# A new order of all four engines' operations in a batch attention

## The chip, the cores and the metric

The kernel runs on one core of a Trainium2 chip. The metric is the time of one execution on the device in microseconds; the lower the better. A core has four compute engines with instruction queues of their own: TensorE (PE for its matmuls, PEld for its weight loads), VectorE (DVE), ScalarE (ACT) and GpSimd (POOL); SyncE (SP) issues most of the DMAs. An engine runs its own list strictly in the order in which the program issued it, and lists meet only at semaphores: `wait_ge(sem, n)` holds an engine until the semaphore has reached n.

## What is computed

Two layers over 32 sequences of 256 tokens with 128 features, each block followed by a layer norm of the sum:

```python
x = _layernorm(x + _L0_attn_ref(x, ...))   # causal attention with relative positions, 16 heads
x = _layernorm(x + _L0_ffn_ref(x, ...))    # 14 routed experts, top 2, and 2 shared
x = _layernorm(x + _L1_attn_ref(x, ...))   # recurrence and feed-forward
x = _layernorm(x + _L1_ffn_ref(x, ...))    # attention over the batch, then 8 experts
```

Only the attention inside the last block matters here. It reads the 32 sequences as the sequence axis: at each of the 256 positions the 32 batch entries attend to one another, causally, with 16 heads of size 8.

```python
s, b, h = x.shape                    # 32, 256, 128
hn = layernorm(x, ln1_w, ln1_b)
q, k, v = jnp.split(hn @ in_proj_w.T + in_proj_b, 3, axis=-1)      # 16 heads of 8
scores = jnp.einsum('sbnd,tbnd->bnst', q, k) / np.sqrt(HEAD_DIM)   # 32 x 32, causal
probs = jax.nn.softmax(scores, axis=-1)
attn = jnp.einsum('bnst,tbnd->sbnd', probs, v).reshape(s, b, h)
x1 = x + attn @ out_proj_w.T + out_proj_b
hn2 = layernorm(x1, ln2_w, ln2_b)    # then router and experts
```

## The kernel before

The program is a row of stages with a barrier of all engines between them. The stage that is changed is `attend_batches` (lines 2623 to 3145). It starts near 1500 us of the span and ends near 1838.

**Groups and steps.** The work is cut into NT = 64 groups `g` of 128 rows (4 positions times 32 batch entries; NPG = 4). Four groups (SLOTS = 4) are a step `f`; there are STEPS = 16 steps, and `g = 4f + s`.

**What a step does once.** `prepare(f)` (ScalarE, line 2957) scales four groups of rows, `turn(f)` (TensorE, 2849) transposes them, `affine(f)` (ScalarE, 2962) makes `hn`. From `hn` come `value` (TensorE, 2871), queries (2855) and keys (2857), which are `project` before. `values_out` (ScalarE, 2993) copies the values, and SyncE's `spread_values` writes them to DRAM and reads them back in another layout; `place_values` (POOL, 2763) makes block-diagonal values of them in two halves. `place_queries` (ScalarE, 2968, four instructions) and `place_keys` (VectorE, 3055, four instructions) do the same for queries and keys.

**What each group does.** `scores` (TensorE: mask 2861, four products 2864) fills the one bank `s_bank`; `soften` (VectorE) takes the maxima (3068) and subtracts them (3070); `exponents` (ScalarE, 2980); `sums` (VectorE, 3061 and the reciprocal 3063); `normalise_probs` (POOL, 2752); `turn_probs` (TensorE, 2879) into the one bank `p_bank`; `probs_out` (ScalarE, 2976) into the one tile `prob_t`; `mix` (TensorE, 2888) into the one bank `o_bank`; `outputs_out` (ScalarE, 2987, four instructions); `output` (TensorE, 2901) into `x_bank`; `add` (VectorE, 3093), `spread` (3098) and `aggregate` (3102) for the moments.

**What follows a step.** POOL's `root` (2728, 2730), `normalise_rows` (2740) and `add_rows` (2734); TensorE's `turn_rows` (2821), ScalarE's `move_rows` (2998), TensorE's router `score` (2828, eight matmuls of eight columns, issued ahead of the output of a step's first group) and VectorE's `keep_logits` (3074). Once, at group 25, `bias_of_experts` runs 32 matmuls of one column (2842). In steps 8 to 15 POOL also scales one expert's weights (`scale_expert`, 2748). `centred`, `e_x`, `prob` and `recip` are double buffers by `g % 2`; `total` and `peak` are single.

**The order** is written out by hand, one `step` function for each engine. Before the change every engine does, for each of the four `s`, a fixed list: TensorE `turn_probs(g-2)`, `scores(g)`, something that the step needs once, `mix(g-2)`, `output(g-3)`. So the scores are two groups ahead of the mix. VectorE does `sums(g-1)` and then `soften(g)`. After the stage come `choose_pairs` and `route_pairs`, which run the experts.

## Time and profile before

| | us |
|---|---|
| median of 3 runs | 2099.05 (2094.2 to 2105.48) |
| the profiled execution | 2104.3 |
| its span, first to last instruction | 2102.6 |
| TensorE busy | 1784.8 (85%) |
| VectorE busy | 1420.5 (68%) |
| ScalarE busy | 1361.6 (65%) |
| GpSimd busy | 1058.8 (50%) |
| mean granted TensorE clock | 0.928 |

The span is some 1.7 us shorter than the time of the same execution. The shares are averages over stages with different limits, so what is said of the changed stage has to be read inside 1500 to 1838 us. Busy time is the time in which at least one instruction of the engine ran. In the timeline each line is a start, a length, the engine and line, and a count of instructions that were merged (`x8`); in square brackets stands the idle time of the engine just before and what ended it. TensorE's instructions overlap, so the distance from start to start, and not the length, says what one costs in a dense row. A float32 matmul stands as two instructions.

### The profile page before, as it was taken

The numbers are of one execution on the slowest core, as the hardware profiler recorded it, in microseconds if no ns is written. First come the engines' busy times: TensorE is split into PE (matmuls) and PEld (weight loads), VectorE is DVE, ScalarE is ACT, GpSimd is POOL, SyncE is SP. The second block draws the span as 40 slices with busy tenths as digits, with TensorE's granted clock in tenths as the row PEclk, the third lists the DMA queues.
The fourth block names the chain that finished last, engine by engine and source line by source line (L and its number), as shares of the span: only waits on it lengthen the run. The fifth ranks groups of instructions, "written<-read, shape, count | busy, mean of one in ns | idle before, by whom it ended". The sixth has DMA issues, their size and how long they took to land. (4 is left out here: it accounts for less than half of the span.)

```text
span 2102.6 us, 52029 instructions
## 1 busy us (share of the span) xinstructions
PE 1784.8 (85%) x15928; PEld 1447.8 (69%) x15928; DVE 1420.5 (68%) x5901; ACT 1361.6 (65%) x3347; POOL 1058.8 (50%) x1384
## 2 busy tenths in 40 slices
PE   7799999999999989889998488888589898748895
PEld 6555555555555558779998377777478888628884
DVE  1377888788787874764422589998377666586775
ACT  3478888888888853324454378887477666416774
POOL 2123333333333323236675788885467777717574
PEclk9799999999999999999999699999799888858998
DMA  7889999999999944025666112221311221258552
GB/s 219 273 275 314 315 307 315 309 314 315 312 312 311 314 149 161 1 64 174 180 198 168 48 45 61 60 60 42 86 35 25 48 46 26 50 83 228 163 183 72
DMA packets 222092, 350.11 MB, mean 167 GB/s; under 512 B 56928, under 2 KB 169568, under 8 KB 221312
## 3 DMA queue, kind: packets, MB, share of 16 engines
q1 hardware_dynamic: 187024, 305.34, 46.1%
q0 software_dynamic: 14144, 31.16, 6.1%
q10 hardware_dynamic: 20656, 10.29, 1.7%
q8 instruction: 137, 2.24, 0.5%
q14 instruction: 131, 1.07, 0.2%
HBM read 160.82 MB, written 144.67 MB: 145 GB/s over the span
## 5 line engine op out<-in xcount | busy, mean ns | idle before, releaser
L183 POOL TENSOR_SCALAR_AFFINE_SELECT heads_raw_relative<-heads_raw_relative 128x508 f32<-128x508 f32 x256 | 167.1, 677 | 502.5 <-ACT heads_raw_relative L568 461.9
L568 ACT COPY heads_raw_relative<-heads_rel_bank 128x768 f32<-128x768 f32 x247 | 198.9, 805 | 124.8 <-PE heads_rel_bank L463 124.6
L492 PE MATMUL attend_turn_bank<-ident,attend_score 128*128 128x128 f32 x1536 | 233.2, 288 | 20.6 <-ACT attend_prob_t L574 20.2
L492 PEld LDWEIGHTS attend_turn_bank<-ident,attend_score 128*128 128x128 f32 x1536 | 164.6, 142 | 118.0 <-ACT attend_prob_t L574 67.9
L574 ACT ACTIVATE attend_prob_t<-attend_turn_bank 128x384 f32<-128x384 f32 x512 | 225.2, 501 | 7.6 <-PE attend_turn_bank L492 7.6
L578 ACT ACTIVATE attend_score<-attend_score,attend_extreme 128x128 f32<-128x128 f32 x512 | 215.6, 421 | 9.0 <-DVE attend_extreme L625 8.7
L625 DVE CUSTOM_DVE_ANT_0 attend_score<-attend_score_bank,heads_relative 128x256 f32<-128x256 f32 x512 | 214.7, 419 | 0.0
L622 DVE CUSTOM_DVE_ANT_0 attend_score<-attend_score_bank,heads_relative 128x128 f32<-128x128 f32 x512 | 146.3, 286 | 77.9 <-PE attend_score_bank L463 51.0
L631 DVE TENSOR_SCALAR attend_score<-attend_score,attend_extreme 128x256 f32<-128x256 f32 x512 | 195.8, 382 | 0.0
L1422 POOL DMA_INDIRECT moe_route_rows_sb<-tokens,moe_taken x154 | 145.9, 948 | 70.1 <-PE moe_route_bank L1444 40.5
L463 PE MATMUL attend_score_bank<-heads_qk 32*128 32x256 f32 x1024 | 156.1, 381 | 0.0
L2583 POOL DMA_INDIRECT recur_got<-expert_out,moe_slots x128 | 137.0, 1070 | 32.1 <-issue 32.1
L463 PE MATMUL heads_rel_bank<-heads_e,heads_qk 32*128 32x256 f32 x988 | 150.8, 382 | 0.0
L460 PE MATMUL heads_rel_bank<-heads_e,heads_qk 32*128 32x128 f32 x988 | 122.9, 325 | 19.4 <-PEq L59 1.5
L1543 DVE COPY moe_route_y<-moe_route_bank 128x128 f32<-128x128 f32 x154 | 44.6, 291 | 130.1 <-PE moe_route_bank L1462 119.8
L460 PE MATMUL attend_score_bank<-heads_qk 32*128 32x128 f32 x1024 | 127.3, 325 | 0.0
L1963 ACT ACTIVATE duo_hid<-duo_hid_bank,duo_w_now 128x128 f32<-128x128 f32 x316 | 98.0, 366 | 40.6 <-PE duo_hid_bank L1924 35.5
L460 PEld LDWEIGHTS heads_rel_bank<-heads_e,heads_qk 32*128 32x128 f32 x988 | 75.2, 186 | 69.6 <-ACT heads_raw_relative L568 47.0
L1933 PE MATMUL duo_y_bank<-moe_w,duo_hid 128*128 x632 | 101.6, 285 | 16.3 <-ACT duo_hid L1963 16.0
L2752 POOL TENSOR_TENSOR batch_prob<-batch_e_x,batch_recip 128x512 f32<-128x512 f32 x64 | 67.1, 1049 | 77.8 <-DVE batch_recip L3063 77.5
L1924 PE MATMUL duo_hid_bank<-moe_z,duo_w_now 128*128 x632 | 103.6, 289 | 2.0 <-ACT moe_z L1956 0.7
L2888 PE MATMUL batch_o_bank<-batch_prob_t,batch_v_blocks 128*128 128x128 f32 x512 | 75.8, 294 | 29.6 <-ACT batch_prob_t L2976 29.6
(434 smaller groups left out, 5327.9 us busy)
## 6 DMA issues: line engine op xcount, KB each, us to landing
shear<-heads_raw_relative SPq DMA_DIRECT2D x128, 768.0 KB, 5.2
heads_relative<-shear SPq DMA_DIRECT2D x128, 768.0 KB, 5.6
duo_w_now<-moe_w SPq DMA_DIRECT2D x158, 129.0 KB
moe_route_w_now<-moe_w SPq DMA_DIRECT2D x154, 129.0 KB
expert_out<-moe_route_y ACTq DMA_DIRECT2D x38, 256.0 KB, 3.4
qk_heads<-heads_qk_out SPq DMA_DIRECT2D x32, 256.0 KB, 4.4
heads_qk<-qk_heads SPq DMA_DIRECT2D x128, 64.0 KB
pair_rows<-groups SPq DMA_DIRECT2D x16, 260.0 KB, 8.0
```

Of the source, the lines that this page charges most:

```text
L183: m = nc.gpsimd.affine_select(out=future, in_=future, compare_op=ALU.is_ge, fill=-BIG, base=1 - P, pattern=[[0, QUAD], [1, P - 1]], channe ...
L460: nc.tensor.matmul(bank[:, 0:P], q[:, 0:P], m[:, 0:P], start=True, stop=True)
L463: mm = nc.tensor.matmul(bank[:, P:W], q[:, P:T], m[:, P:W] if of_rel else m[:, 0:T], start=True, stop=True)
L492: mm = nc.tensor.transpose(bank[:, j * P:(j + 1) * P], score[:, (h - LAG) % RING, j * P:(j + 1) * P], c.ident[:, :])
L568: nc.scalar.copy(raw[:, ring, 2 * half:2 * half + 2, :], r_bank[:, :, 0:W]).then_inc(rel_moved, 1)
L574: nc.scalar.activation(prob_t[:, (h - LAG) % RING, :], bank_of(h)[:, 0:W], ACT.Exp).then_inc(exped, 1)
L578: nc.scalar.activation(score[:, h % RING, 0:P], score[:, h % RING, 0:P], ACT.Identity, bias=extreme[:, h % RING, 0:1], scale=-1.0).then_in ...
L622: nc.vector.tensor_tensor_reduce(score[:, row, 0:P], bank[:, 0:P], rel[:, quad, h % QUAD, 0:P], -SM_SCALE, 3.0e38, ALU.add, ALU.min, extre ...
L625: nc.vector.tensor_tensor_reduce(score[:, row, P:W], bank[:, P:W], rel[:, quad, h % QUAD, P:W], SM_SCALE, -3.0e38, ALU.add, ALU.max, extre ...
L631: nc.vector.tensor_scalar(score[:, h % RING, P:W], score[:, h % RING, P:W], extreme[:, h % RING, 1:2], None, ALU.subtract).then_inc(centre ...
L1422: nc.gpsimd.indirect_dma_start(rows_sb[:, s % TAKEN, :], None, c.tokens, bass.IndirectOffsetOnAxis(ex.taken[:, s // S, s % S:s % S + 1], 0 ...
L2583: nc.gpsimd.indirect_dma_start(got[t % GOT][:, m, :], None, c.expert_out[0:choice.slot_rows, :], bass.IndirectOffsetOnAxis(choice.slots[:, ...
```

## The change

Each engine's `step` gets a new list; no operation is added or left out.

- TensorE: `project` is split into `project_queries` and `project_keys`. In step f it issues the scores of 4f to 4f+3, the turns of probabilities of 4f-4 to 4f-1, and the mixes of 4f-5 to 4f-2, so that scores are up to four groups ahead of the mix. `turn` runs two steps ahead instead of one.
- ScalarE: `outputs_out` and `probs_out` of the last groups stand at the end of the step, around the last `exponents`; `affine` runs two steps ahead.
- VectorE: `soften` of one or two groups stands ahead of `sums`; both halves of `place_keys` stand together between `soften(g+2)` and `soften(g+3)`.
- POOL: `place_values` of a step is done in that step in one piece; `normalise_rows` runs in two pieces that lie a step apart; `add_rows` is moved behind a normalisation.
- New waits say what the old order had implied (`affine` on the last readers of `hn`, `exponents` on `normed`, `soften` on `exped`, `add_rows` on `rooted`), and `total` becomes two buffers.
- The steps run to STEPS + 2, so the work that lags behind is drained by the same lists with conditions.

The diff, cut to its core (the removed lists stand in the listing above):

```diff
-        peak, total = sb("peak", [P, NPG * HB]), sb("total", [P, NPG * HB])
+        peak, total = sb("peak", [P, NPG * HB]), [sb(f"total{u}", [P, NPG * HB]) for u in range(2)]
...
             def add_rows(q):
                 cols = slice(SLOTS * q, SLOTS * (q + 1))
+                pool.wait_ge(rooted, q + 1)
...
+            def normalise_probs(g):
+                u = g % 2
                 pool.wait_ge(recip_done, g + 1)
+                wait_past(pool, p_turned, g - 1)
...
+            def step(f):                                   # POOL
+                g, live = SLOTS * f, f < STEPS
+                if 3 <= f:
+                    normalise_rows(f - 3, 1)
+                if live:
+                    normalise_probs(g)
+                if 2 <= f:
+                    root(f - 2)
+                if live:
+                    place_values(f, 0)
+                    place_values(f, 1)
+                if 2 <= f < STEPS + 1:
+                    normalise_rows(f - 2, 0)
+                if live:
+                    normalise_probs(g + 1)
+                    add_bias(f)
+                    normalise_probs(g + 2)
+                if 2 <= f:
+                    add_rows(f - 2)
+                if 8 <= f < 8 + n:
+                    scale_expert(f - 8)
+                if live:
+                    normalise_probs(g + 3)
...
             def turn(f):
                 pe.wait_ge(z_ready, f + 1)
+                wait_past(pe, hn_ready, f)
...
+            def step(f):                                   # TensorE
+                g, live, more, back, late = SLOTS * f, f < STEPS, f + 1 < STEPS, 1 <= f <= STEPS, 2 <= f
+                if late:
+                    mix(g - 5)
+                if back:
+                    turn_probs(g - 4)
+                if late:
+                    output(g - 6)
+                if live:
+                    scores(g)
+                if more:
+                    project_queries(f + 1)
+                if back:
+                    mix(g - 4)
+                if late:
+                    output(g - 5)
+                if back:
+                    turn_probs(g - 3)
+                if live:
+                    scores(g + 1)
+                if back:
+                    output(g - 4)
+                    turn_probs(g - 2)
+                    mix(g - 3)
+                if live:
+                    scores(g + 2)
+                if more:
+                    project_keys(f + 1)
+                if back:
+                    output(g - 3)
+                if 3 <= f <= STEPS:
+                    turn_rows(f - 3)
+                if back:
+                    mix(g - 2)
+                    turn_probs(g - 1)
+                if live:
+                    scores(g + 3)
+                if f + 2 < STEPS:
+                    turn(f + 2)
+                if more:
+                    value(f + 1)
...
+            def affine(f):
                 act.wait_ge(turned, f + 1)
+                wait_past(act, q_made, f - 1)
+                wait_past(act, k_made, f - 1)
+                wait_past(act, v_made, f - 1)
...
+            def exponents(g):
+                u = g % 2
                 act.wait_ge(softened, soft(g, "centred"))
+                wait_past(act, normed, g - 1)
...
+            def step(f):                                   # ScalarE
+                g, live, more, back = SLOTS * f, f < STEPS, f + 1 < STEPS, 1 <= f
+                if back:
+                    probs_out(g - 3)
+                if live:
+                    exponents(g)
+                if more:
+                    place_queries(f + 1, 0)
+                    place_queries(f + 1, 1)
+                if f + 2 < STEPS:
+                    prepare(f + 2)
+                if back:
+                    outputs_out(g - 3)
+                    probs_out(g - 2)
+                if more:
+                    place_queries(f + 1, 2)
+                if live:
+                    exponents(g + 1)
+                if 3 <= f:
+                    move_rows(f - 3)
+                if live:
+                    exponents(g + 2)
+                if back:
+                    probs_out(g - 1)
+                    outputs_out(g - 2)
+                if more:
+                    place_queries(f + 1, 3)
+                if f + 2 < STEPS:
+                    affine(f + 2)
+                if more:
+                    values_out(f + 1)
+                if back:
+                    outputs_out(g - 1)
+                if live:
+                    probs_out(g)
+                    exponents(g + 3)
+                    outputs_out(g)
...
+            def soften(g):
+                u = g % 2
                 dve.wait_ge(s_made, g + 1)
+                wait_past(dve, exped, g - 1)
...
+            def step(f):                                   # VectorE
+                g, live, more, back, late = SLOTS * f, f < STEPS, f + 1 < STEPS, 1 <= f <= STEPS, 2 <= f
+                if late:
+                    add(g - 6)
+                if live:
+                    soften(g)
+                if late:
+                    add(g - 5)
+                    spread(g - 6)
+                if back:
+                    sums(g - 1)
+                if late:
+                    spread(g - 5)
+                    aggregate(g - 6)
+                if live:
+                    soften(g + 1)
+                if back:
+                    add(g - 4)
+                if live:
+                    sums(g)
+                if back:
+                    spread(g - 4)
+                if late:
+                    aggregate(g - 5)
+                if live:
+                    soften(g + 2)
+                if more:
+                    place_keys(f + 1, 0)
+                    place_keys(f + 1, 1)
+                if back:
+                    add(g - 3)
+                if live:
+                    soften(g + 3)
+                    sums(g + 1)
+                if back:
+                    aggregate(g - 4)
+                if live:
+                    sums(g + 2)
+                if back:
+                    spread(g - 3)
+                    aggregate(g - 3)
```

(The names of the engines behind `def step(f):` are put there for the reader.)

## Rows read from the trace of the kernel before

**Rows 1.** Busy time by stretch: length, then each engine busy, clock, DMA share, GB/s.

```profile
1623.73:1641.17 17.44, 15.72 (x124) 13.91 (x122) 13.41 (x32) 13.87 (x36) 14.52 (x15) 1.00 0.46 90
1686.90:1707.25 20.35, 18.50 (x122) 17.09 (x121) 13.65 (x34) 13.87 (x36) 15.46 (x16) 0.83 0.12 27
...
1516.12:1788.66 272.54, 244.09 (x1660) 221.63 (x1660) 190.16 (x452) 191.21 (x480) 198.06 (x188) 0.89 0.18 40
1828.30:1837.53 9.23, 5.54 (x32) 4.77 (x32) 2.84 (x13) 1.17 (x2) 4.28 (x5) 0.72 0.27 59
```

**Rows 2.** Timeline (start, length, engine, line): the one-column matmuls of group 25.

```profile
1640.35 3.63 PE L2842 MATMUL batch_x_bank<-batch_shift,moe_w 128*128 128x1 f32 x32
```

**Rows 3.** Timeline of TensorE's matmuls, in a stretch of clock 1.00.

```profile
1708.57 1.06 PE L2871 MATMUL batch_v_bank<-fixed_w_in,batch_hn 128*128 128x128 f32 x8
...
1711.18 1.05 PE L2888 MATMUL batch_o_bank<-batch_prob_t,batch_v_blocks 128*128 128x128 f32 x8
...
1712.08 0.39 PE L2901 MATMUL batch_x_bank<-fixed_w_out,batch_out_t 128*128 128x128 f32 x2
...
1712.30 0.60 PE L2879 MATMUL batch_p_bank<-ident,batch_prob 128*128 128x128 f32 x4
...
1712.73 0.38 PE L2861 MATMUL batch_s_bank<-batch_causal,batch_ident_bf 128*128 128x512 bf16 x1
...
1713.84 0.60 PE L2821 MATMUL batch_turn_bank<-ident,moe_z 128*128 128x128 f32 x4
```

**Rows 4.** Waits from 1540 to 1820 us: waiter, releaser, total, times, longest.

```profile
PE batch_o_bank L2888 <- ACT batch_prob_t L2976: 25.9, 17, 1.9
```

**Rows 5.** Timeline: router matmuls of one step, and mix and router of another.

```profile
1636.14 0.96 PE L2828 MATMUL batch_x_bank<-batch_router_now,batch_zt 128*128 128x8 f32 x8
...
1718.95 1.46 PE L2888 MATMUL batch_o_bank<-batch_prob_t,batch_v_blocks 128*128 128x128 f32 x8 [1.85 <-ACT batch_prob_t L2976]
...
1720.20 1.71 PE L2828 MATMUL batch_x_bank<-batch_router_now,batch_zt 128*128 128x8 f32 x8
```

**Rows 6.** Timeline at the stage's end: probability copy, mix, output copy.

```profile
1821.90 0.59 ACT L2976 COPY batch_prob_t<-batch_p_bank 128x512 f32<-128x512 f32 x1
...
1822.54 0.97 PEld L2888 LDWEIGHTS batch_o_bank<-batch_prob_t,batch_v_blocks 128*128 128x128 f32 x8 [0.96 <-ACT batch_prob_t L2976]
...
1823.74 1.06 ACT L2987 COPY batch_out_t<-batch_o_bank 32x128 f32<-32x128 f32 x4 [1.25 <-PE batch_o_bank L2888]
```

**Rows 7.** Timeline of ScalarE, without idle time between.

```profile
1707.92 1.26 ACT L2957 ACTIVATE batch_z<-groups 128x128 f32<-128x128 f32 x4
...
1709.09 1.05 ACT L2987 COPY batch_out_t<-batch_o_bank 32x128 f32<-32x128 f32 x4
...
1710.16 0.59 ACT L2976 COPY batch_prob_t<-batch_p_bank 128x512 f32<-128x512 f32 x1
...
1710.64 0.63 ACT L2980 ACTIVATE batch_e_x<-batch_centred 128x512 f32<-128x512 f32 x1
...
1711.17 0.58 ACT L2993 COPY batch_v_rows<-batch_v_bank 128x512 f32<-128x512 f32 x1
...
1711.63 0.79 ACT L2968 ACTIVATE batch_q_blocks<-batch_q_bank,batch_q_shift,batch_of_b 128x512 f32<-128x512 f32 x1
...
1712.31 1.05 ACT L2987 COPY batch_out_t<-batch_o_bank 32x128 f32<-32x128 f32 x4
```

**Rows 8.** Timeline of VectorE: maxima and centring after the scores of 1712.73.

```profile
1714.04 0.69 DVE L3068 TENSOR_REDUCE batch_peak<-batch_s_bank 128x16 f32<-128x512 f32 x1 [0.16 <-PE batch_s_bank L2864]
...
1714.77 0.69 DVE L3070 TENSOR_TENSOR batch_centred<-batch_s_bank,batch_peak 128x512 f32<-128x512 f32 x1
```

**Rows 9.** Timeline of TensorE: the mask matmuls of groups 0 and 4.

```profile
1511.81 0.59 PE L2861 MATMUL batch_s_bank<-batch_causal,batch_ident_bf 128*128 128x512 bf16 x1 [3.19 <-issue]
...
1528.52 0.39 PE L2861 MATMUL batch_s_bank<-batch_causal,batch_ident_bf 128*128 128x512 bf16 x1 [0.89 <-ACT batch_q_blocks L2968]
```

**Rows 10.** Line 2752's instructions: duration in ns, least, median and most.

```profile
L2752 POOL TENSOR_TENSOR batch_prob<-batch_e_x,batch_recip x64: 1042/1049/1052, 1517.3 to 1821.8; 128x512 f32<-128x512 f32 x64
```

More of the change, by code:

```diff
@@ L2941, in _ @@
+            turn(0)
+            value(0)
+            project_queries(0)
+            project_keys(0)
+            turn(1)
+            for f in range(STEPS + 2):
+                step(f)
             for q in range(STEPS - 3, STEPS):
@@ L3022, in _ @@
             prepare(0)
[L3023 removed]
+            affine(0)
             prepare(1)
             values_out(0)
[L3026 to L3035 removed]
+            for b in range(HB):
+                place_queries(0, b)
@@ L3036, in _ @@
+            affine(1)
+            for f in range(STEPS + 1):
+                step(f)
             for q in (STEPS - 2, STEPS - 1):
@@ L3137, in _ @@
+            for half in range(2):
+                place_keys(0, half)
+            for f in range(STEPS + 2):
+                step(f)
             for q in range(STEPS - 3, STEPS - 1):
```

175 lines of the change are left out of this document (27 added, 148 removed).

## The prediction, made before the changed kernel was run

> **What bounds the kernel now.** I read the busy time and granted clock by stretch first, cut at one recurring instruction of the batch attention (hn, line 2962), so that each stretch is one step of four groups. The reader is to see two kinds of step [rows 1]: one of 17.44 us at clock 1.00, and one of 20.35 us at 0.83. The work of ScalarE (13.87 and 13.87 us busy) and VectorE (13.41 and 13.65) is the same in both; only TensorE's time grows. The starts of line 2962 give six steps of 20.35, one of 25.4 (the one that holds the 32 small matmuls of line 2842, 3.6 us [rows 2]), two near 19.7 and the rest 15.8 to 17.6: 14 steps in 272.54 us [rows 1], 19.5 on average.
>
> Next, the spacing of TensorE's own instructions at the 2.4 GHz level [rows 3], start to start: value, queries and keys together 2.61 (1708.57 to 1711.18), mix 0.90, output 0.22, turn of probabilities 0.43, scores 1.11 (line 2861 to 2821). The other two turns of a step are four transposes as well, 0.44 each; the router's scores (2828) are eight loads and eight matmuls as the mix is, so I take 0.89. One step has 4 x (0.90 + 0.22 + 0.43 + 1.11) = 10.64, and 0.88 + 2.61 + 0.89: **15.0 us**. So 2.4 us of the 17.44 are waits.
>
> Then the waits [rows 4]: the mix waits for ScalarE's copy of the turned probabilities, 25.9 us in 17 waits over 280 us. In the timeline [rows 5] it is one wait of 1.72 to 1.85 us a step, in the last quarter: the mix of group g-2 needs a copy that stands on ScalarE behind work that waited for the maxima. The longer waits of ScalarE for the maxima and of POOL for the reciprocals fall on engines with spare time, and cost only through what they pass on. In a step of the first kind the router matmuls after it took 0.96 us for eight; in one of the second kind 1.71 us, the 1.2 GHz level. The work at that level is what makes 17.44 into 20.35: 2.9 us a step. The engine was idle 1.85 us, and then did eight-column matmuls, when the clock fell. The first fall is in the first step that has router matmuls.
>
> The Trainium skill (TensorE: Matmul & The Clock Gate, "A second HAM failure mode: psum-queue depth-cycling") says that short pauses between groups of matmuls make the clock swing between its levels. The trace agrees, with 0.83 in the steps just named.
>
> **The change part by part.** No operation is removed or added except waits, and a second `total` buffer; it changes what stands behind what. I laid the new step out from the durations above, the handoffs of [rows 6] (start of a probability copy to the mix 0.64 us, which is 0.05 after its end; mix to the first output copy 1.20) and ScalarE's spacing [rows 7]: `prepare` 1.17, output copies 1.07, probability copy 0.48, exponents 0.53, values 0.46, one query placement 0.68.
>
> TensorE: the mix runs four to five groups behind its scores instead of two. With no gap, mix(g-4) starts at 3.5 us of the step, and its probability copy was the last ScalarE item but two of the step before. That copy would start at 17.5 on a clock that begins with the step, so mix may start at 18.2, and TensorE arrives at 15.0 + 3.5 = 18.5. The wait of 1.85 goes, with 0.3 us to spare.
>
> ScalarE: 13.87 us of work in a step of 15.0, so 1.1 to lose. The tightest ring through it: mix(g-4) start, 1.20, output copy 1.07, probability copy 0.48, exponents 0.53, two query placements 1.33, the four of `prepare` 1.17, output copies to output(g-3) 1.11 (1.07 and the 0.05), then TensorE's own 7.9 us to the next mix(g-4): 14.8 us. A ring under 15.0 costs nothing, but it has only 0.2 to spare. The other ring (value, its copy, output copy, probability copy, mix(g), and 10.6 us of TensorE) gives 14.0.
>
> VectorE: 13.65 us. Four softenings must each follow their scores: scores to maxima 1.4 (the weight load before 1712.73 to 1714.04), maxima to centring 0.73, centring 0.69 and the release to the next scores 0.05 [rows 3, 8], 2.9 us in all and 11.5 for four. The 2.9 us of key placement stand between softenings three and four, where TensorE's scores come 3.9 us apart, so they are covered. By hand the last item of the step ends 2.9 us into the next, which is 0.1 past the point where the next scores are ready. The slip is absorbed before score g+1, which has 0.6 to spare.
>
> POOL: 14.52 us in a step without `scale_expert`, 15.46 with it [rows 1]. That is over 15.0 in steps 8 to 15. About 1.5 us of slack ahead of the turns is eaten in three steps, and from then POOL sets about 15.6. I take 15.5 for those steps. POOL's next release is not blocked by its added waits: `p_turned` for g+2 is the turn at 0.9 us of the next step, and the normalisation is at 4.2 of it. Behind that wait on POOL are `add_rows`, `scale_expert` and the last normalisation, whose reader comes at 12.1 of the next step.
>
> Queues: SyncE's order isn't touched. It waits for `v_placed` before it loads the next values; both placements now lie at 11.7 to 15.4 us of the step and the next values are copied out at 16, so nothing queues there. The row writes wait for `rows_normed`, which comes up to a step later, and in their queue only the next value load stands behind them, needed 9 us later. The added waits of `affine`, `exponents` and `soften` are for work one or two steps, or two groups, back: none by the hand schedule. If that cover went, each would hold ScalarE or VectorE by what is missing.
>
> Edges. Scores 0 to 4 took 16.7 us, and from scores 4 to the last addition (1828.30) it was 299.8 [rows 9, 1]. In the new fill, four turns of scores and softening at 2.9 to 3.8 us (the upper with scores at 1.2 GHz, as the first were) give 14.0. In the new tail five mixes, not three, are left after the last scores, 2.3 us apart at the least (1.20 + 1.11) and some 2.9 with the probability copy between: about 17.5 us after scores 63, which start some 11 us after scores 60, so 28.5 from there. After the last addition 9.23 us remain [rows 1], of which 0.6 goes because `add_rows` no longer stands ahead of the last `root`.
>
> **Sum.** From scores 4 to 60, seven steps at 15.1, seven at 15.5, 3.65 for the small matmuls and 2 for a clock fall after them: 219.9. With the 28.5 of the tail 248.4 against 299.8, so 51.4 saved. The fill gives 2.7 and the end 0.6: 54.7. I take off 0.2 us a step for imperfect handoffs: **52 us**. The profiled execution is 2104.3 us (span 2102.6); less 52 is 2052. It lies 5 us above the median 2099.05, so the predicted median is **2047**.
>
> Bounds: all 14 steps at 15.0 (4.2 less) and no discount give 58.9, or 2040. For small waits that I can't see, the bounds are 0 and the 2.4 us now lost in a step of clock 1.00.
>
> **The rivals.**
> A, small waits remain. The ScalarE ring has 0.2 us to spare. With each of its eight links 0.2 longer it is 14.8 + 1.6 = 16.4, and a wait on VectorE's late fourth softening on top could make 17.0. Against 15.3 that is 14 x 1.1 to 14 x 1.7, 16 to 24 us more than forecast: 2063 to 2071, and with a few steps at the low clock up to 2080. For it: the thin margin. Against: durations are steady, and a late TensorE gives ScalarE time. Chance 0.25.
> B, waits moved, not removed. Another wait of about 2 us appears (exponents held by `normed`, or scores held by the late fourth softening, since 2.9 us of keys stand ahead of it) and the clock still falls: steps stay at 19.5, and what the longer tail costs (five mixes instead of three, about 5) and the fill gives (2.7) leaves 2101. Chance 0.07.
> C, slower. Place: ScalarE's end of step, where two output copies and a probability copy now wait on TensorE's next step while TensorE waits for them. If that ring leaves gaps in each of its turns, TensorE may stay at 1.2 GHz. Each microsecond of its 15.0 that runs at the low level adds one. It decides at 4.5 us of such work with nothing hidden (15.0 + 4.5 = the present 19.5). With 7.5 us a step is 22.5: 14 x 3.0 = 42 more, 2141. Against: the hand schedule has no gap over 0.3. Chance 0.06.
> D, POOL held by VectorE. A normalisation on POOL took 1.042 to 1.052 us in all 64 cases [rows 10], whatever VectorE ran beside it. If the sums (0.7 each, as long as the centring) held POOL, a step would be 15.0 + 2.7 = 17.7 and the time near 2082. Chance 0.02. The Trainium skill (SBUF — State Buffer, "SBUF: two separate sides") has such a rule: VectorE with two SBUF inputs or in a two-port mode and GpSimd take one port pair exclusively. The spread of 10 ns shows nothing of it here; if the rule bit on the sums, denser packing would give D.
> That the change doesn't do what it says is out: each list in the diff is issued in that order.
>
> **How the numbers follow.** Forecast 0.60 (own range 2036 to 2060), A 0.25, B 0.07, C 0.06, D 0.02. The range reaches over the forecast and most of A: 2036 to 2074. Half a per cent is 10.5 us, about what a measurement of this kernel can tell from no change. Forecast, A and D are faster: 0.87; B same: 0.07; C slower: 0.06.
>
> **What would show it.** Line 2962 should come every 15 to 15.6 us, with clock 1.00 nearly everywhere; line 2888 should have no wait near 1.8 us; router matmuls (2828) should be eight in about 1 us in every step; POOL should be busy over 95% in steps 8 to 15. Wrong would be: starts over 16.5 us apart, a clock still at 0.83, new waits before lines 2861, 2879 or 2901, or a mean of line 2752 over 1.1 us. A tail over 20 us from the last scores to the last addition would break the edge terms.

## The result, and the profile after

The changed kernel took **2046.43 us** (median of 4 runs, 2042.8 to 2048.84), the kernel before 2096.62 us beside it (4 runs, 2077.07 to 2105.48). The ratio is 0.9755, with a 95% interval of 0.9716 to 0.9793. The forecast was 2047 in a range of 2036 to 2074. The profiled execution took 2048.84 us, 55.5 less than the 2104.3 of before.

The same view as [rows 1], busy time by stretch (length; TensorE matmuls, weight loads, VectorE, ScalarE and POOL busy; granted clock; DMA share; GB/s), of the changed kernel. Each stretch is again one step, from one start of `affine` (now line 2983) to the next, and the last line is 13 steps together:

```profile
1598.53:1613.55 15.02, 15.02 (x123) 13.91 (x122) 13.51 (x34) 13.64 (x36) 14.52 (x15) 1.00 0.17 37
1613.55:1633.64 20.09, 20.09 (x154) 18.98 (x152) 14.08 (x35) 13.88 (x36) 16.05 (x16) 0.92 0.43 80
...
1708.87:1724.27 15.40, 15.40 (x123) 13.86 (x122) 13.89 (x34) 13.70 (x36) 15.32 (x16) 1.00 0.16 36
1523.01:1724.27 201.26, 198.83 (x1560) 182.11 (x1559) 177.14 (x424) 176.37 (x449) 182.52 (x176) 0.99 0.22 46
```

The common step is 15.02 us, and TensorE is busy in all of it (15.02 of 15.02). Of the 13 steps six are 15.01 or 15.02, four are 14.77 to 15.16, and the others are the first (15.75), the one that holds the 32 one-column matmuls (20.09) and the last (15.40). Before, most steps were 17.44 or 20.35. The clock is 1.00 in all of the 13 but the one with the one-column matmuls (0.92). The work of the other engines is as before (VectorE 13.5, ScalarE 13.6 to 13.7); they only stand closer together.

The waits from 1540 to 1740 us, the longest, and one small one that answers to [rows 4]:

```profile
POOL batch_prob L2753 <- DVE batch_recip L3098: 13.3, 14, 4.8
DVE batch_peak L3105 <- PE batch_s_bank L2868: 13.1, 17, 3.8
ACT batch_out_t L3009 <- PE batch_o_bank L2894: 10.4, 11, 1.3
...
PEld batch_o_bank L2894 <- ACT batch_prob_t L2996: 3.5, 14, 0.3
```

TensorE waits little; the long waits left are those of POOL and VectorE, engines with time to spare in most steps. TensorE's matmuls no longer appear on this pair at all (25.9 us and 1.9 at the longest before); its weight loads wait 0.3 us at the longest. ScalarE now waits for TensorE; its wait for the centred scores, 74.4 us in 48 times from 1540 to 1820 us before, is 1.5 us in one. The timeline of the changed kernel shows the two places of [rows 5] anew, the router matmuls and the mix of group g-2:

```profile
1669.85 0.96 PE L2824 MATMUL batch_x_bank<-batch_router_now,batch_zt 128*128 128x8 f32 x8
...
1674.92 1.06 PE L2894 MATMUL batch_o_bank<-batch_prob_t,batch_v_blocks 128*128 128x128 f32 x8
```

Eight router matmuls in 0.96 us, the 2.4 GHz level, and no bracket with idle time behind the mix.

Where the 55.5 us went, by the marks of the forecast's sum (starts of the mask matmuls of groups 0, 4 and 60, then the last addition):

| | before | forecast | after |
|---|---|---|---|
| scores 0 to scores 4 | 16.7 | 14.0 | 13.7 |
| scores 4 to scores 60 | 276.1 | 219.9 (+2.8 taken off the gain) | 215.1 |
| scores 60 to the last addition | 23.7 | 28.5 | 31.9 |
| last addition to the last instruction of the stage | 9.2 | 8.6 | 9.8 |

From here a second measure is of use, the **stage length**: from the first start of `affine` to the first instruction of the next stage (the maxima of line 1704). It is 335.6 us before and 280.3 after: 55.3 of the 55.5 lie in it. It also lets runs on different chips be compared. The first set (e1b, e2, e3, e7) and the third (e1c, e9c and the two kernels again) were made on chips whose time outside this stage is over 100 us longer (the kernel before takes 2247 to 2253 us there); the common steps are the same to 0.02 us. In the table the ratio is always to the kernel before on the same chip. It leaves out executions in the slow state (one of the kernel before's 17 beside the first set, three of 11 beside the second), which the medians in the table contain.

| kernel | stage | common step | time | before beside it | ratio, interval |
|---|---|---|---|---|---|
| before | 335.6 | 17.44, 20.35 | 2096.62 | | |
| before, second trace | 332.0 | 17.44, 20.35 | 2248.83 | 2246.97 | 1.0008 (0.9974 to 1.0041) |
| changed | 280.3 | 15.02 | 2046.43 | 2096.62 | 0.9755 (0.9716 to 0.9793) |
| changed, again | 280.7 | 15.02 | 2208.39 | 2246.97 | 0.9834 (0.9790 to 0.9878) |
| e1b before + filler | 310.3 | 17.45 | 2239.36 | 2253.35 | 0.9948 (0.9911 to 0.9985) |
| e1c the same | 308.4 | 17.44 | 2232.92 | 2246.97 | 0.9943 (0.9913 to 0.9973) |
| e2 extra work in the ring | 298.5 | 16.00 | 2225.49 | 2253.35 | 0.9875 (0.9825 to 0.9926) |
| e3 extra work in the gap | 286.3 | 14.95, 15.43 | 2216.94 | 2253.35 | 0.9838 (0.9787 to 0.9888) |
| e7 one gap | 308.4 | 16.98 | 2238.23 | 2253.35 | 0.9923 (0.9897 to 0.9949) |
| e4 POOL's old order | 291.1 | 15.1 to 17.0 | 2053.25 | 2102.87 | 0.9790 (0.9733 to 0.9848) |
| e5 POOL extra | 291.2 | 15.4, 16.3 | 2053.40 | 2102.87 | 0.9787 (0.9730 to 0.9844) |
| e6 sums first | 287.9 | 15.16 | 2051.39 | 2102.87 | 0.9777 (0.9720 to 0.9834) |
| e8 scale early | 280.7 | 15.02, 15.41 | 2046.63 | 2102.87 | 0.9746 (0.9702 to 0.9790) |
| e9c spread and thin | 276.4 | 15.02 | 2202.46 | 2246.97 | 0.9799 (0.9754 to 0.9843) |

### The profile page after: what moved, and what is told of

It is laid out like the page before. It is cut to its first block and busy times, and to the rows that moved or that the text cites. A ratio compares the mean times of both kernels' runs of the same rounds, so it can differ in the third digit from the quotient of the medians.

```text
span 2046.8 us, 52138 instructions
## 1 busy us (share of the span) xinstructions
PE 1752.1 (86%) x15928; PEld 1417.6 (69%) x15928; DVE 1418.8 (69%) x5901; ACT 1357.5 (66%) x3347; POOL 1056.0 (52%) x1384
## 3 DMA queue, kind: packets, MB, share of 16 engines
q14 instruction: 132, 1.08, 0.2%
## 5 line engine op out<-in xcount | busy, mean ns | idle before, releaser
L622 DVE CUSTOM_DVE_ANT_0 attend_score<-attend_score_bank,heads_relative 128x128 f32<-128x128 f32 x512 | 146.7, 287 | 78.2 <-PE attend_score_bank L463 52.2
L1933 PEld LDWEIGHTS duo_y_bank<-moe_w,duo_hid 128*128 128x128 f32 x632 | 86.7, 199 | 18.1 <-issue 17.7
L1888 POOL DMA_INDIRECT duo_rows_sb<-pair_rows,pair_take x64 | 63.8, 997 | 64.1 <-POOLq L59 45.0
```

What stands on the lines that cost most here:

```text
L622: nc.vector.tensor_tensor_reduce(score[:, row, 0:P], bank[:, 0:P], rel[:, quad, h % QUAD, 0:P], -SM_SCALE, 3.0e38, ALU.add, ALU.min, extre ...
L1933: mm = nc.tensor.matmul(y_bank[u % 3][:, 0:D], hid[u % DEEP][:, k, :], w, start=k == 0, stop=k == 1)
```

## The experiments

In the diffs below, comments such as `# e2` are put there for the reader. Steps are lengths between starts of `affine`, if nothing else is said. The last `affine` runs in step 13, so these lengths do not show the last two steps.

### What the waits and what the clock are worth: a filler in the wait of before

The kernel before, with seven matmuls whose result nobody reads ahead of the mix that waited 1.85 us:

```diff
+                    if s == 3 and not last:
+                        pe.wait_ge(v_out, f + 2)
+                        for k in range(7):
+                            nc.tensor.matmul(v_bank[:, 0:D], c.ident[:, :], c.ident[:, :], start=True, stop=True)
                     if back:
                         mix(g - 2)
```

> The kernel before, with seven extra 128-column float32 matmuls (into the values' bank, free at that time, their result is never used) ahead of the mix of a step's last group, where TensorE stands idle for 1.85 us. They take 7 x 0.22 = 1.5 us, so they fit in the wait and delay nothing. Theory (the wait is what the clock falls after): clock 1.00 in all steps, step 17.44 us instead of 20.35, and 272.54 - (14 x 17.44 + 5.1) = 23 us less: about 2075. Rival 1 (the eight-column router matmuls alone let the clock fall, or nothing in the stage does): steps of 20.35 stay, 2097. Rival 2 (the matmuls get in the way): slower than 2097.

Measured: all steps from the fourth on 17.45 us but the one with the one-column matmuls (22.59). One step of it, in the view of [rows 1]:

```profile
1620.00:1637.45 17.45, 17.19 (x134) 15.48 (x136) 13.70 (x33) 13.88 (x36) 14.11 (x15) 1.00 0.15 32
```

The reader is to see the clock: 1.00, where the kernel before had 0.83 in most steps, although the kernel now does more work (134 matmul records a step against 122). The router matmuls are all there. So they alone do not bring the clock down; without the idle stretch ahead of them it stays. The filler both closes the stretch and adds full-size work there; which of the two keeps the clock was not separated.

The stage is 310.3 us, 25 less than the 335.6 before. The whole time gained less, 14 us (ratio 0.9948). To learn why, the kernel before, the changed kernel and the filler were run once more side by side.

> The kernel before once more, for a second trace of it. If the clock falls at fixed places of the program, its steps are the same as in the first trace (six or more of 20.35 us, the first of the longer ones in the first step with router matmuls); if they fall by chance, the count differs, and the spread of its times (2077 to 2110) comes from it: between all steps at 17.44 and all at 20.35 there are 14 x 2.9 = 41 us.

Two steps of this second trace of the kernel before:

```profile
1609.87:1630.22 20.35, 18.63 (x121) 16.98 (x120) 13.73 (x34) 14.66 (x38) 15.70 (x16) 0.83 0.12 27
1691.40:1708.80 17.40, 15.56 (x123) 14.07 (x123) 12.43 (x33) 11.99 (x31) 10.81 (x12) 1.00 0.14 31
```

Both lengths are there again, but at other places. The starts of `affine` give steps of 19.55, 20.34, 20.34 and 19.95 where the first trace had 19.45, 19.93, 17.45 and 17.44; then one of 17.44 and one of 18.6 where the first had 20.35 twice. So in which steps the clock falls is not fixed by the program. In either trace it is under 1.00 in nine of the eleven steps from the first router matmuls on, but not in the same nine. A fall costs up to 2.9 us, and the times of the kernel before spread over 33 us here (23 runs, 2229.5 to 2262.1).

> The kernel before with the seven filler matmuls again, on the same chip as the changed kernel and the kernel before. The steps were all 17.45 in its first run. Theory: 20 to 24 us less than the kernel before where that has its 20.35 us steps, 28 to 32 more than the changed kernel; its times spread less than those of the kernel before.

The filler again gives 17.44 in all common steps, a stage of 308.4 us against 332.0, and a spread of 16 us (12 runs; 29 in the 12 of the kernel before that belong to its second trace). Its step with the one-column matmuls is 20.93 at clock 1.00 here, 22.59 at 0.92 in e1b. The stages differ by 24 us, the profiled executions by 25, the medians by 14 (2246.97 against 2232.92). The 11 between lie in which executions were traced: the one of the kernel before is 6.4 above its median, the one of the filler 4.7 below its own. The mean clock on record for every execution goes with this. Of the 23 of the kernel before the fastest (2229.5) had 0.925, the median one 0.915 and the slowest (2262.11) 0.906; the traced one had 0.910. So its median execution had fewer falls than the traced one; how many of them in this stage is not shown.

> The changed kernel once more, beside the kernel before and the variants on the same chip. Theory: 52 to 55 us less than the kernel before, all of it between the first scores and the last addition (before 316.5 us, changed 260.7).

The changed kernel's stage is 280.7 us, 51.3 less than 332.0, and its profiled execution 2201.62 against 2253.4 for the kernel before, 51.8. Its median is only 38.6 less (2208.39 against 2246.97). In both kernels the traced execution lies 6 to 7 us off the median, in opposite directions. So the expected 52 to 55 came out in the traces, at its lower edge (from the first scores to the last addition it is 313.1 against 260.9, 52.2 less), and not in the medians on this chip.

### One gap put back

```diff
                 if back:
+                    if 2 <= f < STEPS:
+                        pe.wait_ge(exped, g + 3)
                     mix(g - 2)
```

> The changed kernel with one more wait: TensorE's mix(g-2) waits for exponents(g+2) in steps 2 to 15, which gives one idle stretch of about 1.8 us a step, as the kernel before had, but five microseconds behind the router matmuls instead of directly ahead of them. By hand the ring through that wait is 16.9 us. Theory A (an idle stretch of 1.8 us a step is enough for the clock to fall in most steps): 2.9 more, 19.8 us a step, 2113. Theory B (it takes the idle stretch and the small router matmuls side by side): clock 1.00, step 16.9, 2073.

Measured: common steps of 16.98 us (16.9 by hand), with a stage of 308.4, 28.1 more than the changed kernel. That is theory B's number. In the view of [rows 1], a stretch with low clock and one without, and then TensorE's timeline at the first gap and at a later one:

```profile
1606.30:1625.60 19.30, 16.83 (x114) 15.19 (x115) 13.77 (x33) 13.47 (x36) 14.80 (x15) 0.89 0.13 28
...
1659.80:1676.80 17.00, 15.19 (x120) 13.95 (x121) 13.71 (x34) 13.79 (x35) 14.54 (x15) 1.00 0.15 33
```

```profile
1602.43 1.16 PE L2894 MATMUL batch_o_bank<-batch_prob_t,batch_v_blocks 128*128 128x128 f32 x8 [1.84 <-ACT batch_e_x L3004]
...
1604.25 1.91 PE L2868 MATMUL batch_s_bank<-batch_k_blocks,batch_q_blocks 128*128 128x128 f32 x8
...
1673.61 1.16 PE L2894 MATMUL batch_o_bank<-batch_prob_t,batch_v_blocks 128*128 128x128 f32 x8 [1.70 <-ACT batch_e_x L3004]
```

TensorE is idle before the mix in each step, nearly as long as in the kernel before, and right after it the engine has full-size work. The first two gaps, of 1.84 and 1.89 us, each came with a short fall of the clock, one behind the gap and one at its end (the scores at 1604.25 took 1.91 us where they take 1.05 at full clock; the steps are 17.24 at 0.91 and 19.22 at 0.90), and no router matmul of the stage had run by then. So an idle stretch with full-size work on both sides can bring the clock down, and theory B as it was worded, that it takes both, is not what the runs show. After that the clock is 1.00 in nine of the ten steps, all but the one with the one-column matmuls. The fair comparison is by length: of nine gaps of 1.70 or 1.71 us here none came with a fall, of six stretches of 1.72 us ahead of router matmuls in the two traces of the kernel before three were. So what stands behind the gap matters too. Both counts are small, and the gap's place in the step is not the same.

### The ring through ScalarE

Two kernels add the same work to ScalarE, the four scalings of `prepare` once more into a spare tile:

```diff
+            def extra(f):
+                for s in range(SLOTS):
+                    at = SLOTS * f + s
+                    nc.scalar.activation(spare[:, s, :], groups[:, at, 0:D], ACT.Copy, scale=groups[:, at, D:D + 1])
...
                     prepare(f + 2)
+                    extra(f + 2)              # e2
...
                     exponents(g + 3)
+                    if f + 2 < STEPS:
+                        extra(f + 2)          # e3
                     outputs_out(g)
```

> The changed kernel with 1.17 us more ScalarE work in each step: the four scalings of prepare are done once more into a spare tile, directly behind prepare. ScalarE's total goes from 13.6 to 14.8 us, still under TensorE's 15.0. Theory (a ring through both engines sets the bound: mix(g-4), output copy, probability copy, exponents, two query placements, prepare, output copy, output, and on to the next mix(g-4), 14.8 us): the ring becomes 16.0, so the step becomes 15.9 to 16.0, about 13 us more than the changed kernel: 2060. Rival (only the sum of each engine's work counts): step 15.0, 2046 to 2048.

> The changed kernel with the same 1.17 us of extra ScalarE work per step, placed between exponents(g+3) and outputs_out(g), where ScalarE stands idle for 0.75 us while it waits for mix(g). Ring theory: only 1.17 - 0.75 = 0.42 lengthens the ring, 14.8 to 15.2, step 15.2, about 3 us more than the changed kernel: 2049. Rival (the sum of work counts): the same as with the work in the other place. If place does not matter and the ring is wrong in its own way, both come to 16.

Measured: e2 has common steps of 16.00 us, e3 of 14.95 to 14.97 in the three even steps ahead of the one-column matmuls, and the stages are 298.5 and 286.3 us. In those steps the same 1.2 us of work costs a whole microsecond in one place and nothing in the other. Over the whole stage e2 costs 18.2 us against some 13 expected: three early steps are 16.9 to 17.0, and the one with the one-column matmuls is 23.44 at clock 0.78. e3 costs 6.0 against 3, in its last steps and in the drain, the work that is left behind the last scores. One step of e2, then ScalarE's timeline in it:

```profile
1709.60:1725.60 16.00, 15.18 (x120) 13.82 (x121) 13.70 (x34) 14.82 (x39) 15.38 (x16) 1.00 0.15 33
```

```profile
1711.41 1.06 ACT L3015 COPY batch_out_t<-batch_o_bank 32x128 f32<-32x128 f32 x4
1712.49 0.59 ACT L3002 COPY batch_prob_t<-batch_p_bank 128x512 f32<-128x512 f32 x1
1712.97 0.63 ACT L3008 ACTIVATE batch_e_x<-batch_centred 128x512 f32<-128x512 f32 x1
1714.55 1.06 ACT L3015 COPY batch_out_t<-batch_o_bank 32x128 f32<-32x128 f32 x4 [0.94 <-PE batch_o_bank L2895]
```

No engine is full (ScalarE 14.82, POOL 15.38, TensorE 15.18 of 16.00), and still the step is 16.00. ScalarE idles 0.94 us in front of outputs_out(g) for a mix that comes only after its own probability copy. That idle time is inside the ring, and work put into it, as in e3, is free until another engine's slack is used up. The rival, that only each engine's sum counts, would have had both at 15.0.

The number for e3 was 0.25 too high. I had added what the extra exceeds the gap by, 0.42, to the 14.8 of the ring through the mix. But that ring doesn't pass the extra; the one that does is ScalarE's own list, 13.7 + 1.2 = 14.9, and it is under 15.0. In its last steps e3 comes to 15.43, POOL's length. Its exponents of a step's first group are later against POOL's list, so the slack (next section) is smaller: it is used up when the normalisation starts 3.4 us after those exponents, in the changed kernel at 4.5.

### POOL's slack

```diff
+                if 2 <= f < STEPS:                # e5
+                    nc.gpsimd.tensor_scalar(spare[:, :], causal_f[:, 0:2 * P], factor_of[:, 0:1], None, ALU.mult)
                 if live:
                     normalise_probs(g + 3)
```

> The changed kernel with one more POOL instruction of 0.95 us (128x256) in each step from 2 on, its result is not used. In the changed kernel POOL's own step is 15.4 us in the steps that scale an expert, and yet TensorE's stays at 15.0: POOL falls behind by 0.4 a step and lives on slack. Theory: steps 2 to 7 use 2.4 us of slack, and from step 8 POOL, at 16.4, sets the step: 7 x 1.35 = 9 more, 2055 to 2058. Rival (the slack is much larger, or POOL does not hold anybody): 2046 to 2049.

**Slack** is here how far POOL may fall behind before another engine waits for it. Measured: steps of 15.05 and 15.40 ahead of the one with the small matmuls, and at the end 15.88, 16.30, 16.31 and 16.31. The time is 2053.4, 7 us over the changed kernel's, which was measured on another chip, and the intervals of the two ratios overlap; the stage is 10.9 longer, against 9 expected. One step:

```profile
1697.00:1713.30 16.30, 15.32 (x120) 13.86 (x122) 13.69 (x34) 13.94 (x36) 16.22 (x17) 1.00 0.15 33
```

POOL is busy in 16.22 of 16.30. The first steps with the extra passed without effect, until POOL was some 1.6 us behind; then POOL's 15.40 set the step. In TensorE's long step POOL caught up, and after it two more steps of about 1.3 each passed.

The changed kernel shows the same slack where experts are scaled. The last `exponents` of a step, whose wait ends with POOL's `normalise_probs`, in steps 9, 11, 12 and 13:

```profile
1666.90 0.63 ACT L3002 ACTIVATE batch_e_x<-batch_centred 128x512 f32<-128x512 f32 x1 [0.29 <-POOL batch_prob L2753]
...
1697.72 0.63 ACT L3002 ACTIVATE batch_e_x<-batch_centred 128x512 f32<-128x512 f32 x1 [1.08 <-POOL batch_prob L2753]
...
1713.13 0.63 ACT L3002 ACTIVATE batch_e_x<-batch_centred 128x512 f32<-128x512 f32 x1 [1.47 <-DVE batch_centred L3107]
...
1728.53 0.63 ACT L3002 ACTIVATE batch_e_x<-batch_centred 128x512 f32<-128x512 f32 x1 [1.47 <-POOL batch_prob L2753]
```

The wait is 0.29, 0.69, 1.08 and 1.47 us in the steps 9 to 12 and 1.47 again in step 13; in step 8 there is none. POOL's normalisations start 15.4 us apart from step 8 on, and after four steps the slack is gone. (At 1713.13 the profile names VectorE's centring, but the one that ended then is the next group's; the normalisation ended 0.1 us ahead, as in the other steps.) By the starts of ScalarE's exponents the steps 8 to 11 are 15.02 and the steps 12 to 14 are 15.40. TensorE's scores run ahead of that: by their starts only step 13 is 15.40. In the first group of each of the steps 4 to 8 the normalisation starts 2.88 us after the exponents, before and behind the long step alike, so POOL wasn't behind when the one-column matmuls came, and the long step gave it nothing.

The next kernel takes the small matmuls away from in front of the scaling: `EXPERTS_AT` is 5 instead of 25, and `scale_expert` runs in steps 3 to 10.

```diff
-        FOLD_AT, EXPERTS_AT = 1, 6 * SLOTS + 1
+        FOLD_AT, EXPERTS_AT = 1, SLOTS + 1
...
-                if 8 <= f < 8 + n:
-                    scale_expert(f - 8)
+                if 3 <= f < 3 + n:
+                    scale_expert(f - 3)
```

> The changed kernel with the 32 one-column matmuls taken at group 5 instead of 25 and scale_expert in steps 3 to 10 instead of 8 to 15. POOL's lag then has five steps of 14.5 us to shrink before the end, and the drain after the last scores doesn't wait for POOL. Theory: the last steps stay at 15.0 (15.4 for the last now), the drain loses 1 to 2 us of waits for normalise_probs and normalise_rows; together 2 to 3 us less than the changed kernel, 2043 to 2045. Rival (the drain is bound by its own chain of mixes and copies): 2046 to 2047.

Measured: 2046.63 us, stage 280.7: no gain. Behind the step with the one-column matmuls (20.55 at clock 0.83) the steps are 15.85, 14.83, 15.01, 15.02 and 15.10, and then five of 15.41 or 15.42, POOL's own length. As in the changed kernel four scaling steps passed free and those after them paid 0.4 each. With POOL on time again at the end, the stretch from the last `affine` to the next stage is 56.6 us against 58.9, a little more than the 1 to 2 us that the theory gave to the drain; the steps paid it back. Two of the waits, in the second and the fifth scaling step, the same places as 0.29 and 1.47 above:

```profile
1591.53 0.63 ACT L3002 ACTIVATE batch_e_x<-batch_centred 128x512 f32<-128x512 f32 x1 [0.35 <-POOL batch_prob L2753]
...
1637.79 0.63 ACT L3002 ACTIVATE batch_e_x<-batch_centred 128x512 f32<-128x512 f32 x1 [1.48 <-POOL batch_prob L2753]
```

They show how POOL holds the rest. `exponents(g)` may write `e_x` only when `normalise_probs(g-2)` has read it.

### POOL's old order, and sums first

POOL's list alone put back to the old one, the other three engines in the new order:

```diff
+            def step(f):
+                for s in range(SLOTS):
+                    normalise_probs(SLOTS * f + s)
+                    if s == 0:
+                        place_values(f, 1)
+                    if s == 3 and f + 1 < STEPS:
+                        place_values(f + 1, 0)
+                        add_bias(f + 1)
...
```

> The changed kernel with POOL's list alone put back to the old order (half of place_values behind the first normalisation, the other half of the next step's and add_bias behind the fourth, root and normalise_rows in one step). The next step's values are loaded only at about 23.6 us, so place_values waits for them near 1.2 us in front of the next normalisation: POOL 14.7 + 1.2 = 15.9 us, and 16.8 with scale_expert. Theory (POOL's order is part of the gain): step 15.9 to 16.8, 13 to 25 us more than the changed kernel: 2059 to 2071. Rival (only the order of TensorE, ScalarE and VectorE matters): 2046 to 2049.

Measured: steps that alternate, 17.01, 15.08, 16.73 and 15.10, and with scaling 15.50 and 16.31; stage 291.1, 10.8 more than the changed kernel, against 13 to 25 expected; the time is 7 more, across chips, with overlapping intervals. By the stage POOL's order is part of the gain, under what was expected. The reason given was wrong in its detail: in the timeline `place_values` starts the moment the normalisation before it is done, with no wait for the values. What POOL waits for is the reciprocal:

```profile
1698.40 1.05 POOL L2753 TENSOR_TENSOR batch_prob<-batch_e_x,batch_recip 128x512 f32<-128x512 f32 x1 [0.76 <-DVE batch_recip L3099]
```

The last experiment of this kind puts VectorE's `sums(g + 1)` back ahead of `soften(g + 3)`.

```diff
                 if live:
-                    soften(g + 3)
                     sums(g + 1)
+                    soften(g + 3)
```

> The changed kernel with one VectorE pair put back: sums(g+1) ahead of soften(g+3), so one group's maxima less stands ahead of the sums. The fourth centring comes 0.9 us later; the next step's first scores wait for it, by 0.1 to 0.2 us over the slack. Theory (TensorE bound with little slack there): step 15.1 to 15.2, 2048 to 2049. Rival (maxima ahead of sums is what the gain rests on): step 16 or more, 2060 and over.

Measured: steps of 15.16 us, as expected, and 2051.39 us, 2 more than expected. The stage is 7.6 us longer, of which the other steps explain 1. Another 1.6 us is in the step with the small matmuls (21.66 at clock 0.84 against 20.09 at 0.92), 0.8 in one early step (16.59 against 15.75) and 4.2 behind the last `affine`, in the drain. Why the drain takes so much of it stays open. The maxima ahead of the sums are worth 5 to 8 us of the 55, not the gain.

### A better version

> The changed kernel with the 32 one-column matmuls spread, four ahead of each output of groups 6 to 13, and one expert scaled in each of the steps 5, 6, 8, 9, 11, 12, 14 and 15. Runs so far gave POOL a slack of about 1.6 us in even steps and a lag of 0.39 us for each step that scales; with this spacing the lag stays under 1.6. Theory: no step over 15.1 but those with small matmuls (15.5 to 16), the 20.1 us step gone, the clock fall of 1.4 us in it too, and 1 to 2 us less in the drain: 3 us less than the changed kernel. Rival (the drain is bound by its own chain): 1.4 us less.

```diff
-        FOLD_AT, EXPERTS_AT = 1, 6 * SLOTS + 1
+        FOLD_AT, EXPERTS_AT = 1, 3 * SLOTS + 1
...
-                if 8 <= f < 8 + n:
-                    scale_expert(f - 8)
+                if f in SCALED:                   # (5, 6, 8, 9, 11, 12, 14, 15)
+                    scale_expert(SCALED.index(f))
...
-                if g == EXPERTS_AT:
-                    bias_of_experts()
+                if EXPERTS_AT - n < g <= EXPERTS_AT:
+                    bias_of_experts(g - EXPERTS_AT + n - 1)     # four of the 32 matmuls
```

Measured: 2202.46 us, the changed kernel 2208.39 beside it and the kernel before 2246.97. The stage is 276.4 us against 280.7. The 20.1 us step is gone (15.92 and 16.80 where the small matmuls are now), and all steps after 6 are 15.01 or 15.02:

```profile
1756.00:1771.00 15.00, 15.00 (x122) 13.89 (x121) 13.49 (x34) 13.74 (x36) 14.92 (x16) 1.00 0.17 37
```

That is the 3 us expected and a little more, 4.4 in the trace. The intervals of the two ratios overlap (0.9754 to 0.9843 and 0.9790 to 0.9878), so it is the trace and not the timing that shows it. The drain is 57.8 us from the last `affine` to the next stage against 58.9, and the additions wait for outputs there as long as in the changed kernel (9.4 against 9.3 us). This does not decide for the rival, that the drain is bound by its own chain of mixes and copies: experts are scaled in the steps 14 and 15, so POOL is as far behind at the last exponents as in the changed kernel (4.50 us from the exponents of group 60 to their normalisation in both, 3.42 in e8), and e8 has the shorter drain.

## Why the prediction was right, step by step

**TensorE's 15.0 us.** Right: the common step is 15.02, from the spacing of instructions of [rows 3] alone. The mix's wait went as said.

**The clock.** Right: 1.00 in all steps from the third on but one, and e1b shows its share. Of the kernel before's 272.5 us in 14 steps the filler took 24.4, with no change of order; from there to the changed kernel are another 34 (14 x 2.43). The two parts, kept clock and removed waits, are of like size. What the engine did before the clock fell (an idle stretch, then eight-column matmuls) was read rightly for the kernel before, but e7 shows two falls behind an idle stretch without such matmuls, so they are not a condition. What the Trainium skill says of short pauses between groups of matmuls, that they make the clock swing between its levels (TensorE: Matmul & The Clock Gate, "A second HAM failure mode: psum-queue depth-cycling"), holds for the kernel before; e7, with nine pauses of 1.70 or 1.71 us and no fall behind any of them, shows that such a pause does not bring it down each time.

**The ring of 14.8.** Borne out: with 1.2 us more in it the step is 16.0 (e2), with the same work beside it 15.0 (e3). That no other path of this length exists was not shown. The small margin of 0.2 us, which carried rival A's chance of 0.25, was enough. The 0.2 us a step taken off for imperfect handoffs were not needed (2.8 us).

**POOL at 15.5 in the steps with scaling.** This term was mis-sized. POOL's own length was nearly right (15.4) and so was the slack of 1.5 us (1.6 in the changed kernel, e5 and e8). But the sum charged all seven steps with 0.5 us over 15.0, 3.5 us, though the text beside it had three of them free. Measured by the exponents, four steps were free and three took 15.4: 1.2 us. Between scores 4 and scores 60 only 0.4 of it shows, because the scores run ahead; the other 0.8 falls into the tail (scores 60 to exponents 60 are 5.44 us, 4.62 in the even steps).

**The small matmuls.** 3.65 and 2 us forecast; 20.09 - 15.02 = 5.07 measured.

**The edges.** The fill was 13.7 (14.0). The tail was mis-sized: 31.9 us from scores 60 to the last addition, not 28.5, and the end 9.8, not 8.6. From scores 63 to the last addition it is 20.04 us, not 17.5, just over the 20 that the prediction named as breaking its edge terms. The hand layout of the tail was a chain of TensorE and ScalarE; in the trace POOL works without a break from 1722 to 1771.7 us, and ScalarE's exponents wait 2.08 and 2.17 us for it in the last two steps.

**How the errors add up.** The tail and the end cost 4.6 us more than forecast (3.4 and 1.2). The steps from scores 4 to 60 cost 4.8 less (POOL's 3.1, the small matmuls' 0.6, the rest the 0.1 us over 15.0 that was laid on seven steps and early steps under 15.0), the fill 0.3 less, and the 2.8 taken off for handoffs was not lost: 7.9 in all. The difference, 3.3 us, is nearly all of what the profiled execution gained over the forecast (55.5 against 52). The median still came out within 0.6 us, because the profiled execution of the changed kernel is 2.4 us above its median where 5 was taken over from the kernel before. That the number is so close is luck; the mechanism is not.

**The rivals.** A, B and C did not come; none of the steps is between 16.3 and 17. D, POOL held by VectorE, can be judged by the durations of line 2753 (was 2752), now that VectorE and POOL lie closer: least, median and most

```profile
L2753 POOL TENSOR_TENSOR batch_prob<-batch_e_x,batch_recip x64: 1043/1051/1072, 1519.5 to 1763.4; 128x512 f32<-128x512 f32 x64
```

The median grew by 2 ns against [rows 10] and the longest by 20. The port rule of the Trainium skill (SBUF — State Buffer, "SBUF: two separate sides"), by which VectorE and GpSimd can shut each other out of a shared port pair, is not seen here. But it is hardly tested: no VectorE instruction of the steps reads two SBUF tensors; they read one, or PSUM and one.

## What to carry to other kernels

When four engines each have less work than the step takes, add up TensorE's start-to-start spacing for the bound, then look for rings: a list of handoffs that passes through in-order queues and returns to its start. Work inside such a ring costs its full length, less the small margin that the ring has, even on an engine with idle time; in the idle time that the ring leaves beside it, it costs nothing until another engine's slack is used up. Count a kept clock as part of the gain of closing a gap. And an engine that is a little over the step's length costs nothing for as many steps as its slack lasts (1.6 us of slack, four steps of 0.4 here). Carry this into the sum, and then look whether it is still behind when the drain starts.

## What the runs showed that was not expected

- The steps in which the clock falls differ between two traces of the same program (for example 17.45 in one, 20.34 in the other, for the same step), and the times of that program spread over 33 us where the filled one spreads over 16. A single trace of such a kernel says what a fall costs, not how many there are in its median execution.
- More work in less time: the filler kernel does seven matmuls more in each step and is shorter by 24 us in the stage.
- The step with the 32 one-column matmuls took 22.59 us at clock 0.92 in one trace of the filler kernel and 20.93 at 1.00 in the other.
- Behind idle stretches of 1.70 or 1.71 us with full-size matmuls after them the clock never fell (nine in e7), with the two of 1.84 and 1.89 us in the same kernel it did. In the kernel before, 1.72 us with eight-column matmuls after it let it fall in three of six.
